# One-core attention and quantised feed-forward kernel: the hand-written order of all five engines rewritten, with some small steps given to other engines

## The reference, cut to what matters

```
x_n = layernorm(x)                                  # x: 4 x 256 x 256, per token (row)
q, k = ctx @ Wq.T + bq, ctx @ Wk.T + bk             # ctx: 4 x 256 x 128
att = softmax(q @ k.T)                              # 4 x 256 x 256
x = x + x_n @ att.T                                 # "x2" in the kernel
h = quant8(layernorm(x))                            # per token: scale 127/max|h|, round
g, v = h @ tern(gate_w).T + gate_b, h @ tern(val_w).T + val_b     # 256 -> 1024
p = quant8(silu(g) * v)                             # per token
x = x + p @ tern(out_w).T + out_b                   # 1024 -> 256
```

## Time and profile before

| what | before |
|---|---|
| median of the 3 timed runs | 60.62 us (60.6 to 60.66) |
| profiled execution, whole | 61.23 us |
| its span in the trace | 59.5 us |
| busy, share of the span: PE, DVE, ACT, POOL | 86%, 81%, 80%, 76% |
| granted TensorE clock | 1.0 in the whole span |
| read from HBM, written | 6.04 MB, 1.05 MB |

### The profile page before, as it was taken

How to read it: one execution, slowest core, us unless ns; L and a number is a source line. 1 busy time by engine, 2 the same in 40 slices (tenths; PEclk the granted TensorE clock), 3 DMA queues, 4 the chain that set the end, 5 groups by cost and what they waited for, 6 DMA issues and landing times.

```text
span 59.5 us, 1140 instructions
## 1 busy us (share of the span) xinstructions
PE 51.0 (86%) x298; PEld 32.6 (55%) x301; DVE 48.3 (81%) x122; ACT 47.6 (80%) x84; POOL 45.0 (76%) x102
## 2 busy tenths in 40 slices
PE   1999993999999699929899988899999998889910
PEld 1768842958888478713323634333473753669800
DVE  3249858887999899997998989898999997997150
ACT  0723927999999999978999684999999999698700
POOL 4970006199789888798879978989999999999900
PEclk9999999999999999999999999999999999999999
DMA  0687989999995000000002000399170199920573
GB/s 0 167 305 285 339 315 392 408 406 414 398 409 219 4 6 11 0 6 0 6 0 44 0 0 15 73 174 178 40 147 0 23 184 180 237 81 0 176 232 121
DMA packets 11069, 8.92 MB, mean 150 GB/s; under 512 B 7604, under 2 KB 9140, under 8 KB 11064
## 3 DMA queue, kind: packets, MB, share of 16 engines
...
HBM read 6.04 MB, written 1.05 MB: 119 GB/s over the span
## 4 chain that ended last, share of the span: by engine, by line
POOL 30%; PE 30%; issue 19%; DVE 10%; ACT 5%; POOLq 0%; ACTq 0%
POOL h L344 6%; PE psG L763 5%; PE psO L940 5%; PE psT L778 5%; PE psT L753 5%; POOL r_cols L276 4%; PE psV L763 4%; PE psH L940 3%; POOL rstd L311 3%; ACT o_early L723 3%; DVE x L485 3%; POOL pgam L325 2%; DVE nmax L467 2%; POOL res L372 2%; POOL w_int L409 2%
## 5 line engine op out<-in xcount | busy, mean ns | idle before, releaser
L572 DVE TENSOR_REDUCE pmax<-prod 128x1 f32<-128x1024 f32 x8 | 9.7, 1210 | 0.1
L707 ACT ACTIVATE sil<-psG,s_gv 128x1024 f32<-128x1024 f32 x8 | 8.9, 1111 | 0.6 <-PE psG L874 0.2
L556 DVE TENSOR_TENSOR prod<-psV,sil 128x1024 f32<-128x1024 f32 x7 | 8.5, 1221 | 0.9 <-ACT sil L707 0.5
L859 PE MATMUL psG<-ter_gate,hT 128*128 128x512 bf16 x31 | 8.0, 378 | 0.8 <-ACT sil L707 0.7
L886 PE MATMUL psV<-ter_val,hT 128*128 128x512 bf16 x26 | 7.0, 382 | 0.2 <-issue 0.2
L940 PE MATMUL psO<-ter_out,pT 128*128 128x256 bf16 x48 | 6.2, 272 | 0.7 <-ACT o_early L723 0.7
L940 PEld LDWEIGHTS psO<-ter_out,pT 128*128 128x128 bf16 x48 | 4.4, 98 | 2.4 <-DVE pT L599 0.8
L694 ACT ACTIVATE hT<-psH,unshift 128x256 bf16<-128x256 f16 x8 | 3.8, 474 | 1.5 <-PE psH L842 1.4
L859 PEld LDWEIGHTS psG<-ter_gate,hT 128*128 128x128 bf16 x32 | 2.7, 96 | 4.0 <-issue 2.0
L664 ACT ACTIVATE p_int<-prod,pqs 128x1024 int16<-128x1024 f32 x4 | 4.6, 1141 | 0.0
L715 ACT CAST pT<-pT_int 128x1024 bf16<-128x1024 int16 x4 | 4.2, 1038 | 0.5 <-DMA pT_int<-p_int 0.5
...
## 6 DMA issues: line engine op xcount, KB each, us to landing
...
```

The lines of the kernel that those rows point to most:

```text
L556: nc.vector.tensor_tensor(prod[:, t % P_RING, :], psV[:], sil[:, t % S_RING, :], ALU.mult).then_inc(prod_done, 1)
L572: nc.vector.tensor_reduce(pmax[:, t:t + 1], prod[:, t % P_RING, :], AX.X, ALU.max, apply_absolute_value=True).then_inc(pmax_done, 1)
L707: nc.scalar.activation(sil[:, t % S_RING, :], psG[:], ACT.Silu, scale=s_gv[:, t, 0:1]).then_inc(sil_done, 1)
L859: nc.tensor.matmul(psG[:, c * HC:(c + 1) * HC], hT[:, t, k, :], w_ter[0][:, k * HID + c * HC:k * HID + (c + 1) * HC], start=(k == 0), stop ...
```

## The change

No arithmetic, tile size, buffer or bank is changed; instructions are put in another order on all engines, and some calls get another engine:

- `bias_parts` from DVE to POOL; `bias_copy` from ACT to DVE.
- `q_out(0)` to DVE and `q_out(1)` to ACT; `k_out(2)`, `k_out(3)` to DVE; `normalise(2)` from DVE to ACT.
- `to_int(0,1)` from ACT to POOL; `to_int(2,0)`, `to_int(2,1)` from POOL to ACT; `clip(0,0)`, `clip(2,0)` from DVE to POOL.
- `centre_x2(4)` from POOL, `centre_x2(6)` from ACT, both to DVE.
- `p_round_int`: 0 goes to ACT, 4 and 5 to POOL; `p_round(6)` from POOL to ACT; `widen(3)` to ACT, `widen(4)`, `widen(5)` to DVE; `gamma_p(4)`, `gamma_p(6)` to DVE, 5 and 7 to POOL; both `p_round_half` on ACT and both `p_copy_half` on DVE.
- The loads have a new order on SP: x of batches 0 and 1, the second half of ctx and one part of xt now go ahead of the gate weight, the out weight is last.

The new lists of the transfers, of ScalarE, of the end of GpSimd and of the end of TensorE:

```diff
-            load_ctx(0, 0, 1); load_ctx(1, 1, 2); load_w(0, 0); load_x(0, 0, 2); load_w(0, 1);
-            load_ctx(2, 2, 4); load_x(1, 2, 4); load_x(2, 4, 6); load_x(3, 6, 8); load_w(1, 0);
-            load_xt(0, 0, 1); load_xt(1, 1, 2); load_bo(); load_w(1, 1); load_w(2, 0); load_xt(2, 2, 3);
-            load_w(2, 1); load_xt(3, 3, 4); turn_r(1); turn_r(2); turn(0); turn(1); turn(2); turn(3); turn(4);
+            load_ctx(0, 0, 1); load_ctx(1, 1, 2); load_x(0, 0, 2); load_x(1, 2, 4); load_ctx(2, 2, 4);
+            load_xt(0, 0, 1); load_w(0, 0); load_w(0, 1); load_w(1, 0); load_x(2, 4, 6); load_x(3, 6, 8);
+            load_xt(1, 1, 2); load_xt(2, 2, 3); load_w(1, 1); load_xt(3, 3, 4); load_bo(); load_w(2, 0);
+            load_w(2, 1); turn_r(1); turn_r(2); turn(0); turn(1); turn(2); turn(3); turn(4); turn(5); store(0);
...
+            p_round_int(3); add_bias(4); scale_out(2); scale_out(3); add_bias_shift(5); gamma_p(5);
+            p_round_int(4); p_round_int(5); scale_out(4); add_residual(0); add_bias_shift(6); add_residual(1);
+            scale_out(5); gamma_p(7); scale_out(6); scale_out(7); add_residual(2); add_residual(3);
+            add_residual(4); add_bias_shift(7)
...
+            k_out(0); k_out(1); q_out(1); exps(0); exps(1); abs_sum(0, 0); abs_sum(0, 1); abs_sum(1, 0);
+            att_copy(0); exps(2); att_copy(1); exps(3); normalise(2); abs_sum(1, 1); normalise(3); att_copy(2);
+            load_silu(); att_copy(3); centre_x2(3); to_int(1, 0); to_int(1, 1); h_copy(0); abs_sum(2, 0);
+            centre_x2(5); centre_x2(7); silu(0); h_copy(1); abs_sum(2, 1); h_copy(2); silu(1); to_int(2, 0);
+            h_copy(3); silu(2); to_int(2, 1); h_copy(4); silu(3); p_round_int(0); h_copy(5); silu(4);
+            p_round_int(1); h_copy(6); silu(5); widen(0); p_round_int(2); silu(6); h_copy(7); widen(1);
+            scale_product(0); silu(7); scale_product(1); widen(3); scale_product(2); p_round(6);
+            scale_product(3); p_round_half(0); p_round_half(1); scale_product(4)
...
+            biases(4); value(4); h_transpose(6); gate(5); biases(5); value(5); gate(6); h_transpose(7);
+            biases(6); value(6); last_product(0); gate(7); biases(7); last_product(1); value(7);
+            last_product(2); last_product(3); p_transpose(6); last_product(4); last_product(5);
+            p_transpose_half(0); p_transpose_half(1); last_product(6); last_product(7)
```

More of the change, by code:

```diff
@@ L312, in std_x2, with bias_parts @@
                                         ALU.pow).then_inc(rstd2_done, 1)
+            def bias_parts():
+                pool.wait_ge(l_bh, 16)
+                rest = bh_sb[:]
+                for i in range(NPART - 1):
+                    if i:
+                        pool.wait_ge(bh_step, 2 * i)
+                    same(bh_part[:, i, :], rest).then_inc(bh_step, 1)
+                    pool.wait_ge(bh_step, 2 * i + 1)
+                    nc.gpsimd.tensor_tensor(bh_rest[:, i, :], rest, bh_part[:, i, :], ALU.subtract).then_inc(bh_step, 1)
+                    rest = bh_rest[:, i, :]
+                pool.wait_ge(bh_step, 2 * NPART - 2)
+                same(bh_part[:, NPART - 1, :], rest).then_inc(bh_step, 1)
             def h_step(g):
@@ L436, in _, with bias_copy @@
             nc.vector.memset(r_cols[:], 0.0).then_inc(c_fill, 1)
[L438 to L450 removed]
+            def bias_copy():
+                dve.wait_ge(rows_ps, 1)
+                nc.vector.tensor_copy(bias_rows[:], psO[:]).then_inc(rows_sb, 1)
             def q_out(b):
@@ L472, in invert_sum @@
                 nc.vector.reciprocal(resum[:, b, :], esum[:, b, :]).then_inc(resum_done, 1)
-            def normalise(b):
-                dve.wait_ge(resum_done, b + 1)
-                for m in range(TB):
-                    nc.vector.tensor_scalar(prob[:, b, m, :], prob[:, b, m, :], resum[:, b, m:m + 1], None,
-                                            ALU.mult).then_inc(norm_done[b], 1)
             def add_x(t):
@@ L600, in widen @@
                                       pT_int[:, t % I_RING].rearrange("p k m -> p (k m)")).then_inc(pT_sb[t], 1)
-            def p_round_half(i):
-                dve.wait_ge(pqs_done, LAST + 1)
-                part = prod[:, LAST % P_RING, i * HC:(i + 1) * HC]
-                nc.vector.tensor_scalar(part, part, pqs[:, LAST:LAST + 1], MAGIC_H, ALU.mult,
-                                        ALU.add).then_inc(round_half[i], 1)
-            bias_parts(); q_out(1); stats_x(0, 2); row_max(0); row_max(1); stats_x(2, 4); invert_sum(0);
@@ L609, in _ @@
-            q_out(2); invert_sum(1); gamma_w(0); stats_x(4, 6); scales_w(0); q_out(3); row_max(2);
-            stats_x(6, 8); row_max(3); invert_sum(2); normalise(2); add_x(0); clip(0, 0); invert_sum(3);
-            add_x(1); stats_x2(0); stats_x2(1); mean_x2(0); add_x(2); mean_x2(1); stats_x2(2); add_x(3);
-            mean_x2(2); stats_x2(3); gamma_w(1); mean_x2(3); centre_x2(2); h_max(0); h_max(1); scales_w(1);
-            h_inv(0); scales_h(0); add_x(4); add_x(5); clip(0, 1); stats_x2(4); stats_x2(5); mean_x2(4);
@@ new lines, in _ @@
+            q_out(0); stats_x(0, 2); stats_x(2, 4); row_max(0); row_max(1); q_out(2); k_out(2); k_out(3);
+            q_out(3); invert_sum(0); bias_copy(); invert_sum(1); row_max(2); row_max(3); gamma_w(0);
+            scales_w(0); stats_x(4, 6); stats_x(6, 8); add_x(0); invert_sum(2); stats_x2(0); add_x(1);
+            mean_x2(0); stats_x2(1); invert_sum(3); mean_x2(1); add_x(2); add_x(3); h_max(0); stats_x2(2);
+            stats_x2(3); h_inv(0); gamma_w(1); mean_x2(2); mean_x2(3); scales_w(1); clip(0, 1); centre_x2(2);
@@ L623, in _ @@
+            p_max(4); times_value(5); gamma_p(4); invert_gamma_p(4); clip(2, 1); p_max(5); times_value(6);
+            invert_gamma_p(5); p_max(6); gamma_p(6); widen(2); times_value_half(0); invert_gamma_p(6);
+            times_value_half(1); p_max(7); widen(4); invert_gamma_p(7); widen(5); p_copy(6); add_residual(5);
+            p_copy_half(0); p_copy_half(1); add_residual(6); add_residual(7)
         @block.scalar
@@ L658, in normalise, with p_round @@
                                          scale=resum[:, b, m:m + 1]).then_inc(norm_done[b], 1)
+            def p_round(t):
+                act.wait_ge(pqs_done, t + 1)
+                nc.scalar.activation(prod[:, t % P_RING, :], prod[:, t % P_RING, :], ACT.Identity, bias=magic_h[:],
+                                     scale=pqs[:, t:t + 1]).then_inc(pround_done[t], 1)
             def p_round_int(t):
@@ L682, in att_copy @@
                 nc.scalar.copy(attT[:, b].rearrange("p k m -> p (k m)"), ps_att[b]).then_inc(att_sb, 1)
-            def bias_copy():
-                act.wait_ge(rows_ps, 1)
-                nc.scalar.copy(bias_rows[:], psO[:]).then_inc(rows_sb, 1)
             def h_copy(t):
```

91 lines of the change are left out of this document (32 added, 59 removed).

## The result

The changed kernel takes 61.66 us (median of 4 runs, 61.44 to 62.02), the kernel before 60.64 (4 runs, 60.6 to 60.99; the fourth was taken with the changed kernel): ratio 1.0161, 95% interval 1.0101 to 1.0222. The profiled execution took 62.02 with a span of 60.3 us.

The account below looks back on a forecast made before the run. No engine's work alone bounds the middle stages; ScalarE's list order and waits do. Terms -0.55 - 0.15 - 0.25 + 1.8 = +0.85 put `add_residual(7)` at 57.7, span 60.35; 61.45 on the median, stated as 61.4, range 60.2 to 62.2.

Parts of the forecast that it names:

- the seesaw behind `silu(7)`: Tail: product on TensorE fills psO, ScalarE reads it, next product starts; 1.75 to 1.8 us a step, 61.4 us, chance 0.52.
- stage 1: Up to `att_copy(0)`: 0.55 us earlier, at 14.05 and not 14.60, with `bias_parts` on POOL at no cost.
- stage 2: `att_copy(0)` to `silu(0)`, ruled by ScalarE's list: 0.35 us shorter, 0.15 counted, `silu(0)` at 27.45.
- stage 3: `silu(0)` to `silu(7)`, the loop on one psG: 20.6 us against 20.85, 0.25 shorter, `silu(7)` at 48.05.
- stage 4: `silu(7)` (start S) to `add_residual(7)`: 1.8 us longer, from S + 7.84 to S + 9.65.
- the prediction's own signs of being wrong: Wrong if `silu(7)` before 47.3, products 2-4 not waiting for o_early, or last residual waiting over 0.3 us for `add_bias_shift(7)`.
- energies 0 and 1 done at 8.85, as before: TensorE before `att_copy(0)`: energies 0 and 1 unmoved at 8.85, then four projections to 10.65 and spreading to 11.4.
- `widen(3)` and `p_round(6)` fit into ScalarE's gaps: Tail: both calls, about 1.05 us each, run on ScalarE while TensorE multiplies, with nothing over.
- The faster one: Front gains enough to pay the tail: `silu(7)` at 47.2, `att_copy(0)` 0.85 us earlier than forecast; 60.2 us, chance 0.20.
- that of no change: Gains in front and loss behind cancel: `silu(7)` at 47.2 or a seesaw step of 1.5 us; 60.6 us, chance 0.11.
- GpSimd's list: Tail: POOL's calls, ending at 57.6 with `add_bias_shift(7)`, hold the last residual; 62.1 us, chance 0.17.
- The rule of the Trainium skill: Improve the busiest engine first: TensorE's work stays at 51.04 us, so the change would do nothing.

Follow-up runs that it names:

- Run 1: Changed lists up to about `silu(2)`, those of the kernel before behind, with `to_int(2,0)` and `to_int(2,1)` on ScalarE, three `add_bias` on GpSimd: 60.92 us, ratio 0.9989.
- run 3: Changed kernel with `p_round_int(2)` ahead of `widen(0)` on ScalarE: 61.23 us, ratio 1.0062 to the kernel before.
- run 4: Changed kernel with the turn of tile 3 ahead of that of tile 2 on SP: 62.04 us, ratio 1.0131 to the kernel before.
- run 6: Changed kernel with a second PSUM bank from product 3 on and `p_round_int(2)` ahead of `widen(0)`: 60.93 us, ratio 0.9992 to the kernel before.
- Run 5: Changed kernel with second bank from product 3, `p_round_int(2)` ahead of `widen(0)`, and `add_bias_shift(7)` ahead of `add_residual(2)` on GpSimd: 61.83 us, ratio 1.0146.
- run 2: Changed kernel with `ALT = 3` for 5, so product 3 goes to a second bank: 61.59 us, ratio 1.0067 to the kernel before.
- run 7: To run 6: `invert_gamma_p(6)` earlier, `gamma_p(7)` on DVE with `invert_gamma_p(7)` behind `p_max(7)`, `p_round(6)` ahead of `scale_product(2)`: 60.63 us, ratio 0.9977.
- run 9: Changed kernel with the loads in the order of the kernel before: 65.17 us, ratio 1.0597 to the kernel before.
- run 8: Kernel before with `ALT = 3`, a second bank from product 3 on: 61.02 us, ratio 0.9955.
- run 10: Kernel before with the loads in the order of the changed kernel, all lists old: 64.84 us against 60.97, no interval.
- run 11: Kernel before with `bias_parts` first on GpSimd and `bias_copy` on DVE behind `invert_sum(1)`: 61.41 us, ratio 1.0049.

## Why the prediction was right, and where it was right by luck

The forecast, the seesaw behind `silu(7)`, is what happened: slower, `silu(7)` earlier, the tail longer. The time forecast was 61.4 and the median is 61.66; the span 60.35, and it is 60.3. The sum was +0.85 on the last residual, and the trace has 57.70 - 56.83 = +0.87. That agreement is better than its terms:

| term | predicted | measured |
|---|---|---|
| stage 1, `att_copy(0)` | -0.55 (14.05) | -0.88 (13.72) |
| stage 2 | -0.15 (13.4) | -0.69 (12.85) |
| stage 3 | -0.25 (20.6) | -0.25 (20.60) |
| stage 4, tail | +1.8 (S + 9.65) | +2.69 (S + 10.53) |

The gain in front was forecast 0.87 us too small and the loss behind 0.89 too small. That these two errors cancel is luck. Two of the prediction's own signs of being wrong showed: `silu(7)` at 47.17 lies before 47.3, and product 2 waited for a `widen` and not for o_early. Products 3 and 4 did follow the reads of psO, 1.79 us apart.

**Stage 1** was undersized at one step ("as before" is not exact either, the energies ended at 9.04 before): "energies 0 and 1 done at 8.85, as before". The timeline of the kernel after has them 1.3 us earlier than that:

```profile
5.59 1.92 PE L775 MATMUL psT<-kT,qT 128*128 128x256 f32 x8
7.56 1.10 PE L760 MATMUL psG<-ctx_sb,wqk_sb 128*128 128x256 f32 x4
...
9.46 0.82 PE L785 MATMUL psO<-bh_part,pick 4*128 4x512 bf16 x3
...
12.61 0.58 PE L828 MATMUL psH<-asum,ones 128*128 128x1 f32 x4 [0.41 <-ACT abs_junk L680]
```

In the kernel before `q_out(1)` stood behind `bias_parts` on DVE (6.74) and `k_out(1)` behind an `abs_sum` on ScalarE (7.33); I had both moves in the lists and did not carry them to the energies. The part of ctx was usable by 7.56, against 7.6 forecast. The bias parts on GpSimd took 4.5 us (4.20 to 8.67; estimate 4.8) and were ready before the spreading. Then ScalarE's own list ruled, and no energy: `abs_sum(0,1)` ended at 12.46, TensorE's weight sum waited 0.41 for it with `att_transpose(0)` behind, and `att_copy(0)` started on that at 13.72, after the third `abs_sum` (end 13.5).

**Stage 2**: the idle half microsecond of ScalarE went completely (0.03 left; I had kept 0.2), and its busy time fell by 0.2 where I had it rise by 0.1. The forecast's terms add up to 0.2 shorter (0.1 more work, 0.3 less idle time), where it writes 0.15. `clip(0,0)` took 1.04 (estimate 1.1). DVE's `add_x(4)` did wait 0.45 us for `std_x(4,8)` behind it on GpSimd, but ScalarE, which ruled the stage, did not.

**Stage 3**: exact in sum and within 0.08 for each round (3.54, 2.72, 2.87, 2.86, 2.63, 3.00, 2.98). It was counted call by call. Run 1 shows what hangs on that: one call at a wrong place costs a round 0.5 us, and my 21.3 for that run missed two such rounds, by 1.0 us.

**Stage 4** is where a size was off, by 0.9. The seesaw's own size is right: with the late turn out of the way (run 3) steps of 1.78 and S + 9.52, against 1.75 to 1.8 and S + 9.65. What I left out is ahead of it: the sentence "`widen(3)` and `p_round(6)` fit into ScalarE's gaps" takes tile 3 as turned by then. In the new list `p_round_int(2)` is behind `widen(0)`, the issue of a turn takes SP 1.23 us, and SP goes in order, so two turns were issued late; each then took 4.5 us and not 3.2, so the widens were late, and products 2 and 3 with them. Run 3 removes 1.0 us by exchanging two calls and run 4 only 0.4 by exchanging the turns. The bank gives less than it seems in the changed kernel: without the late turn, adding the second bank moves the last residual only from S + 9.52 to S + 9.43 (runs 3 and 6), since the `widen` on ScalarE and then `p_round(6)` are late next. In time run 6 is 0.3 us faster than run 3 by the medians (the intervals of their ratios overlap), of which the trace of the tail explains 0.1; the rest is left open (the front of run 6's profile was 0.35 earlier, `att_copy(0)` at 13.33, with the same lists).

**The rivals.** The faster one and that of no change needed `silu(7)` at 47.2, and it came at 47.17 (0.33 us of it from stage 1 and 0.54 from stage 2); both fell all the same, since the tail took back more than I had priced: it was the forecast's mechanism that held, with a longer tail. GpSimd's list did not set the end: it ended at 57.35 (forecast 57.6) and nobody waited. Run 5 shows how close that rival was, through a resource that I did not have in it: the stores in SP's list.

The rule of the Trainium skill, page "Perfetto Trace Analysis", section "Identifying the Most-Contended Engine", that the busiest engine is the one to improve, would have given no change as the prediction read it; TensorE's busy time stayed at 51.0 us and the time moved by 1.6%. No run here bears that rule out, since nothing was taken off TensorE.

What stays open, first, is why the turns of tiles 2 and 3 took so long. In all eight kernels with the new end of the lists (the changed one and runs 2 to 7 and 9) these two took 4.0 to 4.9 us; in the five with the old end (the kernel before, runs 1, 8, 10 and 11) no turn took more than 3.6. In the changed kernel the transfer breaks off in the middle. GB/s moved from 46.0 to 47.5, in 40 slices:

```profile
GB/s 218 191 184 157 82 61 34 20 14 0 0 0 0 0 0 0 0 0 0 0 0 0 0 0 7 7 7 7 7 7 14 7 7 14 7 7 14 14 7 7
```

One thing coincides: a transfer of 16 KB on another queue, which the profile calls "instruction", starts near 45.4, with the turn of tile 2 under way and that of tile 3 about to be issued. In the kernel before it starts near 44.3, when only the last 0.4 us of a turn is left. In each of the eight kernels it starts with at least 2.8 us of the flight of one of the two turns still to come, in the five with at most 0.6. No run moves it alone, so whether it is the cause isn't shown.

Also open: why the front of one and the same list differs by up to 0.6 us between profiles (`att_copy(0)` at 13.33 to 13.93). The landing of x of batch 1 moved with it, from 6.28 to 7.07 us (it is the largest piece of the chain there), but no run changed that alone.
